# Fused layernorm, attention and FP8 feed-forward on one core: three steps of the row pipeline put into other units, two temporaries exchanged, a reordered start

## What is computed

```
qkv = xn @ w_qkv.T + b_qkv                      # 16 heads of 16
att = softmax(causal(q k^T / 4 + position bias per head))
out = x + (att v) @ w_proj.T + b_proj
        + (e4m3(xn_bf16 / s_in) @ e4m3(kernel / s_k)) * (s_in * s_k) + bias
```

## Time and profile before

| | us |
|---|---|
| median of 3 runs | 776.4 (774.78 to 777.29) |
| time of the profiled execution | 775.78 |
| its span | 774.0 |
| TensorE busy | 745.4 (96%) |
| VectorE busy | 634.2 (82%) |
| ScalarE busy | 581.6 (75%) |
| GpSimd busy | 531.3 (69%) |

### The profile page before, as it was taken

How to read it: one execution, slowest core, us unless ns; L and a number is a source line. 1 busy time by engine, 2 the same in 40 slices (tenths; PEclk the granted TensorE clock), 3 DMA queues, 4 the chain that set the end, 5 groups by cost and what they waited for, 6 DMA issues and landing times.

```text
span 774.0 us, 23381 instructions
## 1 busy us (share of the span) xinstructions
PE 745.4 (96%) x6413; PEld 503.3 (65%) x6413; DVE 634.2 (82%) x2399; ACT 581.6 (75%) x1263; POOL 531.3 (69%) x525
## 2 busy tenths in 40 slices
PE   7989999999999999999999999999999999999997
PEld 4666566666766667676666767666676766667555
DVE  4898798888889888888988888898888889878723
ACT  4457888787788878778877877887787787877672
POOL 8345767686776768776776777677687767767581
PEclk9999999999999999999999999999999999999999
DMA  6432344435334433533543353344335334433301
GB/s 180 178 138 91 121 174 153 126 117 180 121 128 173 151 126 117 182 124 123 173 151 126 118 183 125 119 173 151 129 119 182 127 115 172 152 109 118 120 32 62
DMA packets 55313, 105.67 MB, mean 137 GB/s; under 512 B 10420, under 2 KB 30388, under 8 KB 55284
## 3 DMA queue, kind: packets, MB, share of 16 engines
q1 hardware_dynamic: 53968, 104.52, 37.9%
q10 hardware_dynamic: 1316, 0.80, 0.4%
HBM read 18.42 MB, written 8.90 MB: 35 GB/s over the span
## 4 chain that ended last, share of the span: by engine, by line
PE 76%; DVE 8%; ACT 7%; issue 5%; DMA 1%; DVEq 1%; SPq 1%; POOLq 0%; ACTq 0%; POOL 0%
PE misc_a L673 15%; PE misc_a L557 13%; PE misc_b L557 10%; PE scoreT_b L647 10%; PE scoreT_a L647 5%; PE score_c L624 4%; PE score_a L624 3%; PE misc_b L673 3%; PE misc_b L608 3%; ACT qk_parts L900 2%; PE scoreT_b L650 2%; DVE row_max L1098 2%; DVE qk_parts L1086 1%; PE scoreT_a L650 1%; PE misc_b L600 1%
## 5 line engine op out<-in xcount | busy, mean ns | idle before, releaser
L1316 POOL TENSOR_SCALAR_AFFINE_SELECT probs<-probs 128x512 f32<-128x512 f32 x256 | 160.4, 637 | 194.6 <-ACT probs L1010 191.7
L1098 DVE CUSTOM_DVE_ANT_0 score_b<-score_b,causal_mask_q 128x384 f32<-128x384 f32 (+3 forms) x321 | 162.8, 524 | 90.8 <-PE score_b L624 72.0
L1098 DVE CUSTOM_DVE_ANT_0 score_a<-score_a,causal_mask_q 128x512 f32<-128x512 f32 x319 | 174.8, 564 | 3.7 <-PE score_a L624 3.6
L1098 DVE CUSTOM_DVE_ANT_0 score_c<-score_c,causal_mask_q 128x256 f32<-128x256 f32 (+3 forms) x384 | 172.2, 476 | 0.0
L1010 ACT ACTIVATE probs<-scoreT_b 128x384 f32<-128x384 f32 (+1 forms) x256 | 132.3, 517 | 45.8 <-PE scoreT_b L650 21.6
L1010 ACT ACTIVATE probs<-scoreT_a 128x512 f32<-128x512 f32 (+1 forms) x256 | 143.4, 560 | 9.4 <-PE scoreT_a L650 8.7
L1098 DVE DVE_READ_ACCUMULATOR2_ANT row_max<- 128x1 f32 x1024 | 143.5, 140 | 0.0
L1010 ACT ACTIVATE probs<-scoreT_c 128x384 f32<-128x384 f32 (+1 forms) x256 | 133.9, 523 | 1.4 <-PE scoreT_a L647 0.9
L673 PE MATMUL misc_a<-probs,v_ones 128*32 128x128 f32 (+3 forms) x1536 | 129.5, 440 | 3.6 <-DVE xnT_lo L1080 2.1
L647 PE MATMUL scoreT_b<-stacks 64*128 64x384 f32 (+3 forms) x320 | 120.7, 396 | 1.4 <-ACT probs L1010 1.3
L624 PE MATMUL score_b<-stacks 64*128 64x384 f32 (+3 forms) x321 | 116.0, 393 | 0.0
(11 more groups left out here) (236 smaller groups left out, 1957.3 us busy)
## 6 DMA issues: line engine op xcount, KB each, us to landing
stacks<-qk_parts SPq DMA_DIRECT2D x128, 512.0 KB, 3.7
x_ring<-in_L_attn_x SPq DMA_DIRECT2D x16, 512.0 KB, 3.6
attn<-out_T SPq DMA_DIRECT2D x63, 128.0 KB, 2.6
xn<-recips SPq DMA_DIRECT2D x31, 256.0 KB
out<-x_ring SPq DMA_DIRECT2D x15, 512.0 KB, 3.0
stacks<-neg_max_T SPq DMA_DIRECT2D x128, 4.0 KB
low_features<-neg_max_T SPq DMA_DIRECT2D x126, 4.0 KB
low_features<-probs SPq DMA_DIRECT2D x8, 128.0 KB, 4.3
```

What stands on the lines that cost most here:

```text
L1098: last = V.tensor_tensor_reduce(bank, bank, CMQ[:, T - w:T], 1.0, LEAST, ALU.add, ALU.max, MX[:, g % 2, 8 * h + 4 + qt:8 * h + 5 + qt])
L1316: last = GP.affine_select(out=d, in_=d, compare_op=ALU.is_ge, fill=0.0, base=0, pattern=[[0, HU], [1, P]], channel_multiplier=-1)
```

## The change

- `invert` moves from (0, 8) to (1, 3). On SyncE the load of the next row's first stacks goes ahead of `store_recips`, and `load_max(b, 2)` ahead of `spread_recips`.
- The statistics move from (1, 3), (1, 6), (1, 7) to (2, 6), (2, 9). `rstd` moves on GpSimd from ahead of `mask(b, 2, 0)` to behind `mask(b, 2, 1)` and `ffn_bias`. The first `normalise` moves from (3, 1) to (3, 2).
- The parts of `quant_magic` move from (2, 1), (2, 2), (2, 3) to (1, 6), (1, 6), (1, 7). QE becomes the memory of VS, the value rows, instead of XN: part 0 waits for `va_ready` instead of `div_done`, the evacuation of the values waits for `qm_done`, and `normalise` and the last spread no longer do.
- At the start, the two `job_V(0, i)` move from the first unit's chunks to chunks 1 and 3 of the second; `job_T(1)`, the bias projection and VectorE's parts of them move to other chunks, and two fillers (`warm_halves`) fewer run.

```diff
-NORM_AT = [(3, 1), (3, 3), (3, 4), (3, 6)]
+NORM_AT = [(3, 2), (3, 3), (3, 4), (3, 6)]
-INVERT_AT, LAST_INVERT_AT = (0, 8), (2, 11)
+INVERT_AT, LAST_INVERT_AT = (1, 3), (2, 11)
-STATS_AT, AGGR_AT = [(1, 3), (1, 3), (1, 6), (1, 6)], (1, 7)
-MAGIC_AT, FIRST_MAGIC_AT = [(2, 1), (2, 2), (2, 3)], [(0, 1), (0, 3), (0, 4)]
+STATS_AT, AGGR_AT = [(2, 6), (2, 6), (2, 9), (2, 9)], (2, 9)
+MAGIC_AT, FIRST_MAGIC_AT = [(1, 6), (1, 6), (1, 7)], [(0, 1), (0, 3), (0, 4)]
...
-        QE = XN[:, :, :].rearrange("p t c -> p (t c)").rearrange("p (a n) -> p a n", n=T)
+        QE = VS[:, :, :].rearrange("p t c -> p (t c)").rearrange("p (a n) -> p a n", n=T)
...
-        RB = QE
+        RB = XN[:, :, :].rearrange("p t c -> p (t c)").rearrange("p (a n) -> p a n", n=T)
...
-                    sp.wait_ge(qm_done, 2 * B)
...
-                if not first:
-                    store_recips(b - 1)
                 if not last:
                     wait_alone(sp, (w_loaded, 16), (st_ready, ROW * b + SLOTS),
                                (ql_ready, 4 * (b + 1) + 2))
                     load_stack(b + 1, 0)
                 if not first:
+                    store_recips(b - 1)
+                load_max(b, 2)
+                if not first:
                     spread_recips(b - 1, last)
-                load_max(b, 2)
                 regroup(b, 0, first)
...
-            job_V(0, 0)
             pe.wait_ge(first_pair, 16)
...
-                if n == 5:
-                    job_V(0, 1)
-                else:
-                    warm_halves(1)
+                warm_halves(1)
...
-                if c == 2:
+                if c in (1, 3):
+                    job_V(0, c // 2)
+                elif c == 5:
                     for ct in range(CT):
                         job_T(1, ct)
-                elif c == 8:
+                elif c == 7:
                     project_bias()
...
+                    act.wait_ge(qm_done, 2 * (b + 1))
...
-                    if not (isinstance(b, int) and b == 1):
-                        act.wait_ge(qm_done, 2 * b)
...
-                        wait_alone(dve, (x_loaded, 16), (qk_magic, b + 1), (div_done, b - 1))
+                        wait_alone(dve, (x_loaded, 16), (qk_magic, b + 1), (va_ready, b))
...
-                    if g == 2 and more:
-                        rstd(b + 2)
...
                     if g == 2:
                         ffn_bias(b)
+                    if g == 2 and more:
+                        rstd(b + 2)
```

More of the change, by code:

```diff
@@ L198, in build @@
         kt, ke, km = slabs[:, 4, :], slabs[:, 5, :], slabs[:, 6, :]
-        QE0 = AS[:, 1, :, :]
         kern_raw = XQ[:, 0, :].rearrange("p (a c) -> p a c", c=C)
@@ L958, in _ @@
                 normalise(1, t)
-            for i in range(2):
-                V_evac(0, i)
             max_hi(0, 0)
@@ L966, in _ @@
             A(PH[:, :, :], STB[0][:, :].rearrange("p (a c) -> p a c", c=C), ACT.Copy).then_inc(setup_hi, 1)
+            for i in range(2):
+                V_evac(0, i)
             act.wait_ge(qz_done, 1)
@@ L1114, in quant_magic @@
             def quant_magic(b, part):
-                exponents = QE0 if isinstance(b, int) and b == 0 else QE
                 if part == 0:
-                    if isinstance(b, int) and b < 2:
+                    if isinstance(b, int):
                         dve.wait_ge(qk_magic, b + 1)
+                        dve.wait_ge(va_ready, max(b, 1))
                     else:
-                        wait_alone(dve, (x_loaded, 16), (qk_magic, b + 1), (div_done, b - 1))
-                    V.tensor_scalar(exponents.bitcast(I32), QT.bitcast(I32), 0x7F800000, None, ALU.bitwise_and) \
+                        wait_alone(dve, (x_loaded, 16), (qk_magic, b + 1), (va_ready, b))
+                    V.tensor_scalar(QE.bitcast(I32), QT.bitcast(I32), 0x7F800000, None, ALU.bitwise_and) \
                         .then_inc(qe_done, 1)
@@ L1126, in quant_magic @@
                     ct = part - 1
-                    V.scalar_tensor_tensor(out=QM[:, ct], in0=exponents[:, ct], scalar=E4_LEAST, in1=QM[:, ct],
+                    V.scalar_tensor_tensor(out=QM[:, ct], in0=QE[:, ct], scalar=E4_LEAST, in1=QM[:, ct],
                                            op0=ALU.max, op1=ALU.mult).then_inc(qm_done, 1)
@@ L1193, in _ @@
                                     ALU.subtract).then_inc(setup_lo, 1)
[L1194 to L1197, removed]
+                if c in (8, 10):
+                    T_lo(1, c // 2 - 4)
+                if c == 9:
+                    dve.wait_ge(bp_ready, 1)
+                    V.tensor_tensor(BP[:, :], STB[0][:, 0:C], BP[:, :], ALU.add).then_inc(bp_made, 1)
             def invert_last(g):
```

## The result

| | before | after |
|---|---|---|
| median us (range) | 775.59 (774.76 to 777.29) | 805.1 (802.06 to 807.9) |
| profiled execution, its span | 775.78, 774.0 | 807.9, 806.2 |
| ratio, 95% interval | | 1.0371 (1.0339 to 1.0402) |

The change makes the kernel 3.7% slower, some 29 us. The forecast was 799.8 in a range of 780 to 812. An execution over 1.5% longer than the fastest of its kernel is left out of medians and ratios; the only such ones are three of the five of "quantiser alone", its profiled one (832.8 us) among them.

What follows compares the result with a forecast made beforehand. TensorE, busy 96% of the span, was taken to bound the kernel. Start -1.5, row 0 +0.4, rows 1 to 14 14 x 1.45, row 15 +4.2 gave +23.4 us, thus 799.8, range 780 to 812.

Steps and rivals of the forecast that it cites:

- The chain of the late inverse: Reciprocals, store, SyncE's maxima, spread, `divide`, unit 1's last mask: TensorE's products wait, costing 1.45 us a round.
- 1.2 to 1.6 named as the sign: Expected new TensorE wait for unit 1's last mask on GpSimd, 1.2 to 1.6 us, 14 times.
- the longer wait of L600 for `QK_lo`: Expected sign: the feed-forward job on TensorE waits 0.3 us longer for VectorE's low part of the q/k projection.
- It lies ahead of the mask wait and costs nothing beside it: VectorE's extra work in unit 1 delays the feed-forward job 0.3 us, costing nothing beside the 1.4 us mask wait.
- The third quantiser part: VectorE at (1, 7): one part of 0.61 us replaces the aggregate of 0.31.
- The start: First two units: first ends 0.9 to 1.5 us sooner, second about even; 1.5 us gained, bounds 0.5 and 2.
- Row 0: First round, without the mask wait, so VectorE's delay of the feed-forward job counts in full: +0.4 us in the sum.
- Rows 14 and 15: Last rows: mask waits from late inverses, 1.45 us in row 14 and 4.2 in row 15.
- rival B: Waits in every round let TensorE's clock fall to half: +10 to +21 us more, 810 to 821; chance 0.13.
- rival A: Inverses arrive in time, leaving VectorE's 0.3 us a round and part of row 15: +4.6, 781 us; chance 0.12.

Runs made afterwards that it cites:

- quantiser alone: Kernel before with only the quantiser's three parts moved to (1, 6), (1, 6), (1, 7) and their exponents in the value rows' memory: 809.6 us, ratio 1.041.
- half the bytes: Changed kernel with each of the two spreading DMAs carrying 128 KB instead of 256 KB, so half the output is wrong: 786.4 us, ratio 1.013.
- third part at (2, 1): Changed kernel with the quantiser's third part at (2, 1) instead of (1, 7): 818.8 us, ratio 1.055.
- start alone: Kernel before with only the new order of the start, its loop untouched: 778.2 us, ratio 1.001.
- statistics alone: Kernel before with only the statistics moved to (2, 6), (2, 9), with rstd and the first normalise later: 778.2 us, ratio 1.002.
- quantiser (third part in unit 2) and statistics: Kernel before with quantiser and statistics moved as in the change, but the third quantiser part at (2, 1): 778.5 us, ratio 1.000.
- last rows as before: Changed kernel with the inverse at (0, 8) and SyncE's old order in rows 14 and 15 only: 801.4 us, ratio 1.034.
- inverse alone: Kernel before with only the inverse moved to (1, 3) and SyncE's new order: 822.0 us, ratio 1.059.
- run 29: Not a label but a count: the unchanged kernel before, executed 29 times on one chip, took 773.9 us at clock 0.998 and 780.4 at 0.985.

## Why the prediction was right, and where it was not

- **The chain of the late inverse: right in kind and size.** Place, order and releaser are those of the prediction. In its numbers: `divide` 5.99 us after the issue (forecast 5.7), 1.54 us a round in rows 1 to 13 (1.45). TensorE's idle time is 0.97 in the mean, though, under the 1.2 to 1.6 named as the sign, since TensorE reaches the wait later than before; and the longer wait of L600 for `QK_lo` that was to show this did not come (2.6 us in 13 waits, 2.3 in 12 before): it waits for maxima ahead of it instead. That the bytes are a good part of the 5.99 us is shown by half of them (1.5 us less); what is left at no bytes was not measured. By the Trainium skill, "DMA: Bandwidth & Descriptors", section "Anatomy of one DMA", the pair would land after an estimated 3.3 us and the halved pair some 0.3 us sooner; that fit is given there for DMAs issued by GpSimd, and SyncE issues these. The runs show 1.5 us sooner, so this pair's movement is far slower than that rule has it.
- **"It lies ahead of the mask wait and costs nothing beside it": supported, not isolated.** VectorE's extra alone is 0.38 us a round (half the bytes; forecast 0.3), the whole 1.54, near the 1.45 forecast for the chain alone, and that chain passes through the reciprocals at (1, 3) but not through the parts at (1, 6) and (1, 7). With the third part at (2, 1) the feed-forward job came 0.78 us sooner behind the spread's issue and `divide` no sooner, as this has it; but the part then met `divide`, so the time of that run can't settle it.
- **The third quantiser part: mis-sized.** The prediction gave it 0.61 us of occupancy; it was 0.90, with a mask beside it. Within the change the mask wait seems to cover that. Moving the quantiser without the statistics, or the part to (2, 1) with the inverse late, puts it beside `divide`, where it took up to 2.1 us longer.
- **The start: wrong sign.** Forecast -1.5; alone it is +0.36 in the profile and nothing that can be measured in the median. The first unit did end sooner (the second unit's chunks start at 31.79, forecast 31.9, before 33.43), but the second took 11.6 us (31.79 to 43.40) instead of "about even": values jobs, transposes, bias and VectorE's parts of them now meet in it. Behind it come two waits for maxima (0.46 and 0.44 us in "start alone"). The +1.58 of the changed kernel's profile has in it also the third quantiser part in row 0 (0.62) and half clock (0.60), for which the sum had no term there.
- **Row 0: +0.92 instead of +0.4.** In the kernel with the third part at (2, 1) it is 44.36 against 45.01, so 0.65 of it is that part.
- **Rows 14 and 15: 5.65 (1.45 and 4.2) forecast, 9.7 measured.** The wait of row 15 was near (3.60 us of idle time, forecast 4.2); that of row 14 is 2.33, since `divide` starts 7.5 us after the issue of its spread (713.69 to 721.23); and half clock at both was left out of the sum. It was priced only as rival B, for every round. Part of the 9.7 may not be the change's: the end of the kernel before took 78.6 us with 9.0 of them at half clock, while "start alone", "statistics alone" and "quantiser (third part in unit 2) and statistics", whose last rows wait for no late inverse, took 80.9 to 81.3 with 15.7.
- **Rival B (the clock) was wrong for the loop and right for the ends.** With 0.69 to 1.27 us of idle time a round the clock held in all 13 rounds, and with 0.83 to 1.60 too (last rows as before); with 1.70 to 2.46 us it fell in 6 of 13 (third part at (2, 1)), with 1.55 to 2.97 in 5 of 13 (inverse alone); with 2.3 and 3.6 us in the last two rows it fell at once. The size of the wait alone doesn't decide: a wait of 1.44 us in row 15 had a fall behind it, and some of over 2.3 us in the loop had none. The forecast had only that one wait to go by.
- **A slip in rival A.** Its text says some 2 us for row 15, its sum has 1.5; by its own text it would be 781.5.

The sum of the misses in the profile: start +3.1, row 0 +0.5, loop +1.2, ends +4.0, together 8.8, which is the distance from 799.2 to 807.9 but for rounding. All go the same way, so the forecast was not saved by errors that cancel. The median, 805.1, lies under the profiled execution, which had the lowest clock of the four (0.981 against 0.984 to 0.989).

## What to carry to other kernels

A result that goes through memory and back is as late as its producer plus every instruction that its queue issues in between: move the producer later only if the whole chain (store, the queue's other issues, transfer, consumer, and what stands behind the consumer) still ends ahead of the engine that bounds the kernel. When an instruction with two tensors in SBUF moves to another slot on VectorE, look at what GpSimd runs in that slot, not only at how long the instruction took in the old one. Take a change apart before judging it: here the statistics were free and the start nearly so, the quantiser's third part cost 0.4 to 0.6 us a round wherever no mask wait was there to hide it, and the inverse without the other three was worse (822.0 us) than all four (805.1).

## What the runs showed of the hardware

**VectorE and GpSimd exclude each other.** An instruction of VectorE that reads two tensors in SBUF took 0.69 us alone, 0.98 beside a mask of 0.63, and 2.4 to 2.9 where it started behind `divide` of 2.37, ending 0.55 us after it; GpSimd's three masks then took 0.4 us more together. Where it started just ahead of `divide`, it took its 0.69 and `divide` up to 2.87. Maxima (one input in PSUM) beside `divide` took their usual 0.73. This stood in the trace of before already (VectorE, then GpSimd, 429 to 433 us) and was overlooked:
```profile
429.96 0.91 DVE L1127 SCALAR_TENSOR_TENSOR quant_work<-xn,quant_work 128x512 f32<-128x512 f32 x1
```
```profile
429.69 0.64 POOL L1316 TENSOR_SCALAR_AFFINE_SELECT probs<-probs 128x512 f32<-128x512 f32 x1 [0.91 <-ACT probs L1010]
430.30 2.83 POOL L1355 TENSOR_TENSOR attn_lo<-attn,attn_hi 128x1024 fp32r<-128x1024 f32 x1
```
The part is 0.22 longer than its twin of 0.69, as the mask runs beside it, and `attn_parts` takes 2.83 behind it instead of its usual 2.39. The Trainium skill, "SBUF — State Buffer", section "SBUF: two separate sides", has it as a lock: whichever of the two starts first holds the shared ports for its whole instruction, and the other stands. The traces agree: 2.78 us against 0.69 where `divide` was first, `divide` 2.87 against 2.37 where the part was.

**The time of a kernel follows its clock from one execution to the next.** The kernel before, run 29 times on one chip, took 773.9 us at a mean granted clock of 0.998 and 780.4 at 0.985. At 0.988 to 0.990 it took 777.6 to 779.6, and the changed kernel, on another chip, 802.1 (0.989) and 806.1 (0.988): some 23 to 28 us of the 29 remain at the same clock.
